# Where the last tiles of a routed block collect their expert parts: twelve tiles' loads on SyncE by counted pairs, and the late block's down products among the last pairs

## The reference

```python
x = x + tanh(g_xattn) * cross_attention(layernorm(x), ctx_768, mask)
topk_idx, topk_w = router(layernorm(x))               # 6 of 32 experts for each token
h   = relu2(einsum('th,eih->tei', xn, up_w)) * combine[:, :, None]
moe = einsum('tei,ehi->th', h, down_w)                 # routed experts, 128 wide inside
shared = relu2(xn @ shared_up_w.T) @ shared_down_w.T   # 512 wide inside
x = x + tanh(g_ffn) * (moe + shared)
```

## Time and profile before

| | us |
|---|---|
| median of 3 runs (lowest to highest) | 724.94 (724.51 to 725.96) |
| the profiled execution's own time | 724.91 |
| its span in the profile | 723.0 |
| PE busy in the span | 675.8 (93%) |
| DVE busy | 523.6 (72%) |
| ACT busy | 454.5 (63%) |
| POOL busy | 475.1 (66%) |
| mean DMA rate | 200 GB/s |

### The profile page before, as it was taken

The page is one execution under the profiler, slowest core; times in us unless marked ns, Lnnn a source line. Parts: engine busy times, 40 slices in busy tenths (PEclk is TensorE's granted clock), DMA queues, the critical chain, the costliest instruction groups (busy, mean ns, idle before and its releaser), DMA issues.

```text
span 723.0 us, 18770 instructions
## 1 busy us (share of the span) xinstructions
PE 675.8 (93%) x5928; PEld 570.4 (79%) x5928; DVE 523.6 (72%) x1782; ACT 454.5 (63%) x1299; POOL 475.1 (66%) x478
## 2 busy tenths in 40 slices
PE   7999998899898989889999899999999999999975
PEld 6888887778787878765674799998899888898854
DVE  2676788787878787876473566666568888888887
ACT  1567757688887878782524765656775576665740
POOL 1455442667566666667777777777777777777764
PEclk9999999999999999999999999999999999999997
DMA  8990000252222222443838986666679999999866
GB/s 296 381 285 3 2 2 23 74 213 95 90 94 88 88 96 88 145 155 127 326 118 282 317 279 212 211 192 191 200 238 325 346 351 345 348 352 343 257 202 232
DMA packets 86305, 144.80 MB, mean 200 GB/s; under 512 B 14646, under 2 KB 60993, under 8 KB 85184
## 3 DMA queue, kind: packets, MB, share of 16 engines
q1 hardware_dynamic: 54288, 71.23, 31.3%
q0 software_dynamic: 19968, 52.34, 19.4%
q10 hardware_dynamic: 11952, 20.03, 8.3%
HBM read 78.00 MB, written 69.73 MB: 204 GB/s over the span
## 4 chain that ended last, share of the span: by engine, by line
PE 49%; DVE 23%; ACT 9%; DVEq 9%; issue 6%; DMA 2%; SPq 1%; ACTq 0%
PE ps L1560 8%; PE ps L1575 8%; PE ps L1416 5%; PE ps L1363 5%; PE ps L1546 4%; DVEq L1178 4%; PE ps L1214 3%; PE ps L1334 3%; PE ps L1447 3%; ACT big L606 3%; PE ps L1326 2%; ACT att L606 2%; DMA big<-in_x_t 2%; PE ps L1428 2%; DVE big L1159 2%
## 5 line engine op out<-in xcount | busy, mean ns | idle before, releaser
L470 POOL DMA_INDIRECT routed_rows<-x_n,slots x120 | 122.2, 1019 | 66.8 <-issue 24.8
L560 POOL DMA_INDIRECT token_parts<-hid,place x112 | 115.8, 1034 | 37.5 <-issue 31.7
L1560 PEld LDWEIGHTS ps<-att 128*128 128x128 f32 x768 | 99.9, 191 | 17.4 <-issue 10.3
L712 ACT ACTIVATE att<-ps 128x512 f32<-128x512 f32 x96 | 57.3, 597 | 82.5 <-PE ps L1546 77.7
L1560 PE MATMUL ps<-att 128*128 128x128 f32 x768 | 102.0, 276 | 4.1 <-DVE att L1142 2.1
L606 ACT ACTIVATE att<-ps,nmax,rstd 128x154 f32<-128x154 f32 x176 | 82.9, 502 | 21.7 <-DVE nmax L843 16.1
L725 ACT ACTIVATE att<-big 128x256 f32 x224 | 80.3, 408 | 2.6 <-issue 2.2
L1575 PE MATMUL ps<-big,att 128*128 x300 | 78.3, 384 | 3.3 <-DVE picked L1151 2.9
L1334 PE MATMUL ps<-att,big 64*64 64x128 f32 x1536 | 62.2, 282 | 8.5 <-ACT att L623 3.7
L623 ACT ACTIVATE att<-ps 128x512 f32<-128x512 f32 (+1 forms) x96 | 48.1, 544 | 31.1 <-PE ps L1326 31.1
L1214 PE MATMUL ps<-big,hid 128*128 128x128 f32 x512 | 62.8, 276 | 2.0 <-DMA big<-in_x_t 1.3
(11 more groups left out here) (268 smaller groups left out, 1529.6 us busy)
## 6 DMA issues: line engine op xcount, KB each, us to landing
mid<-routed_rows SPq DMA_DIRECT2D x168, 138.0 KB
big<-token_parts ACTq DMA_DIRECT2D x48, 256.0 KB
routing<-routed_rows SPq DMA_DIRECT2D x56, 138.0 KB
x_n<-token_parts ACTq DMA_DIRECT2D x24, 256.0 KB
routed_rows<-pad_row SPq DMA_DIRECT2D x1, 4416.0 KB
routed_rows<-pad_row SPq DMA_DIRECT2D x32, 138.0 KB
x_all<-in_x SPq DMA_DIRECT2D x4, 1024.0 KB, 12.8
big<-in_x_t SPq DMA_DIRECT2D x4, 1024.0 KB, 14.1
```

The source lines that it names most:

```text
L470: nc.gpsimd.indirect_dma_start(rows, bass.IndirectOffsetOnAxis(ap=slots[:, t, k:k + 1], axis=0), normed(t), None).then_inc(s_sca[t // TB % ...
L560: nc.gpsimd.indirect_dma_start(parts, bass.IndirectOffsetOnAxis(ap=place[:, p // 2 % 8, p % 2 * 2 + j:p % 2 * 2 + j + 1], axis=0), y_sb[p ...
L712: A.activation(xt(p), ps[:, p % 2, :], ACT.Copy).then_inc(s_xts, 1)
L1560: ins = M(ps[:, 2 + p % 2, j * P:(j + 1) * P], w_up[p % 2][:, j, c * P:(c + 1) * P], xt(p)[:, j * 256 + c * P:j * 256 + (c + 1) * P], star ...
```

## The change

- **Loads.** `PART_LOAD` is every second pair from 51 on, for tiles 0 to 29 (51, 53, ..., 109). Tiles 0 to 19 stay on ACT. Tiles 20 to 29 are loaded by SP: 20 to 26 stand among its row loads, behind those of the pair eight ahead; 27, 28 and 29 behind all rows. `N_LAST` is 2: tiles 30 and 31.
- **Counts.** Five counts of eight numbers are read in place of two: ahead of tile 20 (the rows of tiles up to 23), of 24 (up to 25), of 26 (up to 27), and two in a row behind tile 26 (up to 29, and all). They come from a product of the table with ones: five small products more on PE in the table stage; DVE's work for it is some instructions fewer.
- **Shared expert.** 32 tasks in place of 28 among the pairs: `SHARED_STEP` spaces the first 28 by 10/3 in place of 11/3 pairs, and block 7's `down_late` follow at 104, 106, 108 and 110. Up to pair 53 that is 14 tasks (10, 13, 16, 20, 23, 26, 30, 33, 36, 40, 43, 46, 50, 53) where 12 stood (10, 13, 17, 21, 24, 28, 32, 35, 39, 43, 46, 50).

```diff
-PART_READY = {0: DONE[1], EARLY: DONE[2], 12: DONE[3], 16: DONE[4], 20: DONE[5]}
-PART_LOAD = {DONE[1] + 5 + 11 * t // 5: t for t in range(24)}
-PART_LOAD.update({103 + 2 * i: 24 + i for i in range(4)})
+PART_READY = {0: DONE[1], EARLY: DONE[2], 12: DONE[3], 16: DONE[4]}
+PART_LOAD = {DONE[1] + 5 + 2 * t: t for t in range(SEG_END[8])}
-N_LAST = NT - SEG_END[7]
+N_LAST = NT - SEG_END[8]
-SHARED_STEP = {10 + 11 * k // 3: task for k, task in enumerate(LATE)}
+SHARED_STEP = {10 + 10 * k // 3 if k < 28 else 2 * k + 48: task for k, task in enumerate(LATE)}
...
+            def wait_scattered(need):
+                for j in range(8):
+                    sp.wait_ge(s_ys[j], need[j])
             def load_parts(t):
+                if t in SEG_END[4:7]:
+                    wait_scattered(load_counts(SEG_END.index(t) - 3))
                 sp.wait_ge(s_fin, t - 2)
...
                     store(PART_LOAD[p - STORE_LAG])
-            need = load_counts(1)
-            for j in range(8):
-                sp.wait_ge(s_ys[j], need[j])
-            for t in range(SEG_END[5], SEG_END[7]):
-                load_parts(t)
-            need = load_counts(0)
-            for j in range(8):
-                sp.wait_ge(s_ys[j], need[j])
+                if PART_LOAD.get(p - AHEAD, 0) >= SEG_END[4]:
+                    load_parts(PART_LOAD[p - AHEAD])
+            need_most, need_all = load_counts(4), load_counts(5)
+            stored = STORED
+            for p, t in PART_LOAD.items():
+                if p + AHEAD >= N_PAIRS:
+                    while stored < t - 3:
+                        store(stored)
+                        stored += 1
+                    if t == SEG_END[7]:
+                        wait_scattered(need_most)
+                    load_parts(t)
+            wait_scattered(need_all)
...
+            for a, at, cols in ((1, 480, 4), (2, 484, 2)):
+                for i in range(a):
+                    M(ps[0:2, 5, at:at + cols], tiles_bf[:, i, :], ones_bf[:, 0:cols], start=i == 0, stop=False, skip_group_check=True)
+                M(ps[0:2, 5, at:at + cols], tiles_f[0:n, a, :], cst[0:n, C_CUM + NE - 1:C_CUM + NE * cols:NE], start=False, stop=True,
...
-            pe.wait_ge(s_xts, N_PAIRS)
-            for t in range(NT - TB, NT):
-                down_late(t)
```

More of the change, by code:

```diff
@@ L72 @@
 assert (TOPK * P * EARLY - NE * (P - 1)) // P >= 2 * EARLY_PAIRS
-PART_READY = {0: DONE[1], EARLY: DONE[2], 12: DONE[3], 16: DONE[4], 20: DONE[5]}
-PART_LOAD = {DONE[1] + 5 + 11 * t // 5: t for t in range(24)}
-PART_LOAD.update({103 + 2 * i: 24 + i for i in range(4)})
+PART_READY = {0: DONE[1], EARLY: DONE[2], 12: DONE[3], 16: DONE[4]}
+PART_LOAD = {DONE[1] + 5 + 2 * t: t for t in range(SEG_END[8])}
 STORED = sum(p + STORE_LAG < N_PAIRS for p in PART_LOAD)
-N_LAST = NT - SEG_END[7]
-LATE = [(i, s) for i in range(FULL, NBLK) for s in range(8) if i >= GAP or s >= 4][:-TB]
-SHARED_STEP = {10 + 11 * k // 3: task for k, task in enumerate(LATE)}
+N_LAST = NT - SEG_END[8]
+LATE = [(i, s) for i in range(FULL, NBLK) for s in range(8) if i >= GAP or s >= 4]
+SHARED_STEP = {10 + 10 * k // 3 if k < 28 else 2 * k + 48: task for k, task in enumerate(LATE)}
 LAST = NBLK - 1
@@ L212, in flamingo_block @@
         end_i = sb("end_i", [1, NE], I32)
-        used = x_n1[:, 0, 0:N_TILES + 16]
-        need_i = sb("need_i", [1, 16], I32)
+        tiles_by = x_n1[:, 0, 0:6]
+        turn = x_n1[:, 0, 8:16]
+        need_i = sb("need_i", [1, 6 * 8], I32)
         flat = hid[:, :, :, :].rearrange("p a s n -> p (a s n)")
@@ L315, in x2t_bank @@
             return 5 if j == 0 else 4
-        def down_bank(t):
-            return 5 if t < NT - TB else (0, 1, 4, 5)[t % 4]
         def ring_row(p):
@@ L392, in store, with load_counts @@
                 sp.dma_start(out_tiles[t], x_all[:, t, :]).then_inc(s_st, 16)
-            def load_counts(which):
-                low, high = ((NT * TOPK, N_PAIRS), (SEG_END[7] * TOPK, DONE[7]))[which]
+            def load_counts(w):
+                low, high = SEG_END[4 + w] * TOPK, (DONE + [N_PAIRS])[4 + w]
                 sp.wait_ge(s_need, 1)
-                return [sp.value_load(need_i[0:1, 8 * which + j:8 * which + j + 1], min_val=32 * ((low + 15 - 2 * j) // 16),
+                return [sp.value_load(need_i[0:1, 8 * w + j:8 * w + j + 1], min_val=32 * ((low + 15 - 2 * j) // 16),
                                       max_val=32 * ((2 * high + 15 - 2 * j) // 16)) for j in range(8)]
+            def wait_scattered(need):
+                for j in range(8):
+                    sp.wait_ge(s_ys[j], need[j])
             def load_parts(t):
+                if t in SEG_END[4:7]:
+                    wait_scattered(load_counts(SEG_END.index(t) - 3))
                 sp.wait_ge(s_fin, t - 2)
@@ L420, in _ @@
                     store(PART_LOAD[p - STORE_LAG])
-            need = load_counts(1)
-            for j in range(8):
-                sp.wait_ge(s_ys[j], need[j])
-            for t in range(SEG_END[5], SEG_END[7]):
-                load_parts(t)
-            need = load_counts(0)
-            for j in range(8):
-                sp.wait_ge(s_ys[j], need[j])
+                if PART_LOAD.get(p - AHEAD, 0) >= SEG_END[4]:
[11 more added lines that the diff above has]
+            wait_scattered(need_all)
             for i in range(N_LAST):
                 sp.dma_start(sums[:, i, :, :].rearrange("p k d -> p (k d)"), part_tiles[NT - N_LAST + i]).then_inc(s_pl2[i], 16)
-            for u in range(STORED, NT - N_LAST):
+            for u in range(stored, NT - N_LAST):
                 store(u)
@@ L762, in _ @@
                     hidden_late(*SHARED_STEP[p])
-                if p in PART_LOAD and PART_LOAD[p] < SEG_END[5]:
+                if p in PART_LOAD and PART_LOAD[p] < SEG_END[4]:
                     load_parts(PART_LOAD[p])
@@ L918, in add_late @@
                 dve.wait_ge(s_dn2, t - TB * FULL + 1)
-                V.scalar_tensor_tensor(x_all[:, t, :], ps[:, down_bank(t), t % 2 * D:(t % 2 + 1) * D], tanh_g[:, 1:2], x_all[:, t, :],
+                V.scalar_tensor_tensor(x_all[:, t, :], ps[:, 5, t % 2 * D:(t % 2 + 1) * D], tanh_g[:, 1:2], x_all[:, t, :],
                                        ALU.mult, ALU.add).then_inc(s_acc2, 1)
@@ L1102, in _ @@
             V.tensor_copy(exp_i[:], ps[0:1, 5, 256:256 + N_TILES])
+            V.tensor_copy(tiles_by[0:1, :], ps[0:1, 5, 480:486])
+            V.tensor_scalar(turn[0:1, :], iota_e[0:1, 0:8], -2.0, 15.0, ALU.mult, ALU.add)
             dve.drain()
             V.tensor_scalar(row_i[:], tile_key[0:1, :], -1.0, None, ALU.add).then_inc(s_row, 1)
[L1105 to L1111, removed]
+            V.tensor_tensor(need_i[:].rearrange("p (w j) -> p w j", w=6), turn[0:1, :].unsqueeze(1).broadcast_to([1, 6, 8]),
+                            tiles_by[0:1, :].unsqueeze(2).broadcast_to([1, 6, 8]), ALU.add)
             dve.drain()
@@ L1186, in _ @@
                 g = sums[:, i, :, :]
-                add_late(t)
                 dve.wait_ge(s_pl2[i], 16)
@@ L1442, in down_late @@
                     pe.wait_ge(s_h, t + TB)
-                if TB * FULL < t <= NT - TB:
+                if t > TB * FULL:
                     pe.wait_ge(s_acc2, t - TB * FULL)
@@ L1446, in down_late @@
                 for s in range(4):
-                    ins = M(ps[:, down_bank(t), t % 2 * D:(t % 2 + 1) * D], h[:, s, t % TB * P:(t % TB + 1) * P], down_sh[:, s, :],
+                    ins = M(ps[:, 5, t % 2 * D:(t % 2 + 1) * D], h[:, s, t % TB * P:(t % TB + 1) * P], down_sh[:, s, :],
                             start=s == 0, stop=s == 3, skip_group_check=True)
@@ L1520, in _ @@
             ins.then_inc(s_cum, 1)
+            for a, at, cols in ((1, 480, 4), (2, 484, 2)):
+                for i in range(a):
+                    M(ps[0:2, 5, at:at + cols], tiles_bf[:, i, :], ones_bf[:, 0:cols], start=i == 0, stop=False, skip_group_check=True)
+                n = TABLES[a][1]
+                M(ps[0:2, 5, at:at + cols], tiles_f[0:n, a, :], cst[0:n, C_CUM + NE - 1:C_CUM + NE * cols:NE], start=False, stop=True,
+                  skip_group_check=True)
             up(3, 0)
```

## The result

| | kernel before | changed kernel |
|---|---|---|
| median of 4 runs (lowest to highest), us | 725.45 (724.51 to 726.29) | 737.32 (735.16 to 739.90) |
| ratio to before (95% interval) | | 1.0155 (1.0126 to 1.0184) |
| time and span of the profiled execution | 724.91 and 723.0 | 739.90 and 738.1 |

The change makes the kernel 1.5% slower, some 12 us. The direction was predicted, the size was not: the forecast was 731.7, and the range ended at 736. One thing first, so that the profile is read rightly: the profiled execution is the slowest of the four. DVE starts pair 0 at 406.88 us in it, and at 402.75 before; 3.25 of these 4.1 us were already there at 340 us and arose in the first 30, which hold no instruction of the change.

What follows compares the result with a forecast made beforehand. DVE's pace was taken to bound the kernel from about pair 55, PE's before. For DVE's end: 720.9 + 0.6 + 1.9 - 0.4 - 1.5 - 1.1 = 720.4, + 2.1 + 5.2 = 727.7; time 731.7 us, range 727 to 736.

Steps and rivals of the forecast that it cites:

- Table stage: Before pair 0, where PE is the chain: five small products more, three bfloat16 and two float32, cost +0.6 us.
- Two tasks more ahead of pair 54: PE reaches pair 54 3.4 us later, DVE wins back 1.55: +1.9; one late add gone ahead: -0.4.
- The end: Waits for a down product behind the loop (-1.5) and for tile 24 (-1.1) go; moved adds gain nothing.
- step 4: SP's count reads delay part loads: DVE waits 2.1 us for tile 20 and 5.2 for tile 27.
- The anchor: First loads behind the counts of tiles 20, 24 and 26 go out 10.05 us after pairs 90, 98, 102 begin.
- covered: Row loads, 5 us late behind each count, run eight pairs ahead (over 20 us), so they cost DVE no wait.
- the rival of full queues: DMA queues full, PE slow: landings stay 8.3 us, waits 4.8 for tile 20, 9.0 for 27; about 737, chance 0.08.
- its premise that DVE's work is kept: Same 32 tiles of parts and 20 late adds, so only shifts of DVE's start and its waits were counted.
- Hidden reads: Rival: SP's count reads are hidden, tiles 20 and 27 arrive in time; 724.4 us, no change, chance 0.09.
- Faster tail: Rival: DVE has slack in the loop, so the 6 us moved from the end vanish there; about 718, chance 0.05.
- The rule that was weighed: Shared DMA engines agree with moving loads from ACT to SP free; small sequencer time opposes read waits, leaving 724.4.

Runs made afterwards that it cites:

- the first experiment: The changed kernel with all forty of SP's count reads moved ahead, one behind each row load of pairs 48 to 87: 726.85 us, ratio 1.0019 to the kernel before.

## Why the prediction was right or wrong

The forecast for DVE's end was 727.7; measured 735.68 in the profile. In the time it was 731.7 against a median of 737.32.

1. *Table stage, +0.6.* Too large, and small: the chain has the five products in 0.31 us.

```profile
384.71 0.10 PE ps L1527
384.80 0.05 PE ps L1529 x2
...
384.90 0.12 PE ps L1529 x2
```

Ahead of pair 0 the profiled execution is 3.5 us later than the forecast counts, 4.13 in place of 0.6. Of this 3.25 is the start of this execution and 0.5 the first expert products, which PE ran slowly:

```profile
405.19 1.66 PE L1570 MATMUL ps<-big,att 128*128 128x128 f32 x8 [1.55 <-ACT att L733]
```

The eight took 1.13 before. Pair 0 began anywhere from 402.75 to 406.88 in the eleven profiles of this study, whatever the kernel, so beyond the 0.31 none of it is put down to the change.

2. *Two tasks more ahead of pair 54: right.* DVE began pair 54 at 548.84 and pair 55 at 551.67:

```profile
547.95 0.48 DVE L927 SCALAR_TENSOR_TENSOR x_all<-ps,tanh_g,x_all 128x256 f32<-128x256 f32 x1 [1.04 <-PE ps L1451]
548.84 0.42 DVE L1145 TENSOR_SCALAR hot<-ps 128x256 f32<-128x256 f32 x1 [0.41 <-PE ps L1570]
...
551.67 0.42 DVE L1145 TENSOR_SCALAR x_n<-ps 128x256 f32<-128x256 f32 x1
```

Against the earlier trace rows that is 7.71 and 6.08 later; without the 4.13 from ahead of pair 0 it is 3.58 and 1.95, forecast 3.4 and 1.9. A task of the shared expert costs its length where PE sets the pace, and the wait that DVE wins back is worth subtracting. The tasks alone cost 1.4 to 1.7 us, and undoing them gave 0.8 to 1.7; each time the effect is near the limit of what the runs can tell.

3. *The end: half right.* The wait for a down product behind the loop is gone, line 927 never waits for line 1451 from 560 on, and two tiles stand in the tail, 2.2 us each:

```profile
730.67 0.42 DVE L1169 TENSOR_TENSOR x_all<-x_all,x_n 128x256 f32<-128x256 f32 x1
731.19 0.96 DVE L1193 TENSOR_TENSOR big<-big 128x768 f32<-128x768 f32 x1
...
733.40 0.95 DVE L1193 TENSOR_TENSOR big<-big 128x768 f32<-128x768 f32 x1
```

Tile 24's wait did not go (1.78 in pair 102), but step 4 had counted such a wait within its 5.2, so the sum holds no error for that.

4. *SP's reads: the mechanism right, the size too small.* This is the step that failed: the waits of 2.1 and 5.2 us in the sum. Forecast were waits of 2.1 and 5.2; measured 1.5 (tiles 20 and 21) and 7.8 (tiles 24, 26, 27), 9.3 in place of 7.3.
   - The anchor failed. The prediction took the first load behind the counts of tiles 20, 24 and 26 to go out 10.05 us after pairs 90, 98 and 102, "the same place", since SP's row loads wait there for DVE. For 90 and 98 it was right (9.6 and 10.1). At pair 102 SP did not wait for DVE: it had not yet worked off tile 24's count. The 4.6 us of a count were weighed against the 20 us that the row loads run ahead, and "covered" was right for the rows, for which DVE never waited; but the lead that they lose is missing at the next count, four pairs on. The experiment with only tile 24's count moved shows it: there tile 27 goes out 20.4 us after pair 102.
   - The other numbers of that step held. Tile 27's loads went out 10.9 us behind tile 26's (forecast 11.0), it took 4.9 us to the step (4.5), and DVE wanted it 20.6 us after pair 102 (20.4, the waits taken out). 23.5 + 4.9 - 20.6 = 7.8.
   - Tile 20 landed 4.5 us after its issue; the 5.6 I took was too careful. The queues were not full just then: the DMA share is 0.98 from 560 to 680, but 0.73 while tile 20's loads ran (663.9 to 668.4). Tile 21 ran at full share (668.4 to 675) and took 6.6 (668.39 to 675.02). Its wait of 0.98 was not in the forecast.
   - The range was narrower than its own bounds. With 0.9 and 4.8 for tile 20 and 4.0 and 9.0 for tile 27, added to 724.4, they give 729.3 to 738.2, not 728 to 736; the upper end was left to the rival of full queues.

5. *Not in the forecast: DVE's odd iterations.* The step that adds into `x_all` (line 1167, 1162 before) takes 0.48 us in place of 0.42: 26 of 30 times from pair 55 on, where it was 3 of 28 before. All of one shape from 560 to 700, before and then changed (count, busy, mean ns):

```profile
L1162 DVE TENSOR_TENSOR x_all<-x_all,big 128x256 f32<-128x256 f32 x16 | 6.8, 426 | 0.0
```

```profile
L1167 DVE TENSOR_TENSOR x_all<-x_all,big 128x256 f32<-128x256 f32 x16 | 7.7, 480 | 0.0
```

   An odd iteration takes 2.33 in place of 2.27 by this, some 1.6 us over the 26 to 28 of them. This term stood at nothing in the prediction, by its premise that DVE's work is kept: the number of instructions is kept, their length is not. It is in the experiments without waits for parts too (23 of 30 at 0.48 with all reads ahead, 18 of 30 with the loads on ACT), and the tasks alone do it 9 of 28 times. So it comes in part with the tasks and in part with the rest of the change; what does it was not tried, and stays open.

Together, against the forecast for DVE's end: 3.5 ahead of pair 0, 2.0 waits, 1.6 odd iterations, and 0.9 in pieces under 0.5, among them more idle times of 0.2 to 0.5 without a named cause; 8.0 in all. The last two, 2.5 in sum, would also explain that the first experiment stands at 726.85 and not at the 724.4 that the sum gives without new waits. With the 3.5 set aside, 2.0 + 1.6 + 0.9 explain 4.5 of the 5.6 us between the forecast and the median 737.32; the rest of 1.1 lies in executions that left no profile, and would fit such starts, which is argued and not shown. With either the waits or the odd iterations at their forecast the median would have been near 735.5, inside the range; it took both.

*The rivals.* Hidden reads: fallen, by moving them (10.5 us) and by doubling them (24 more). Full queues and a slow PE: the time came out nearest to this rival's 737, yet its mechanism is wrong. Tiles 20, 26 and 27 came 4.5 to 4.9 us after their issue, tile 24 5.2 and tile 21 6.6, none 8.3, and the first experiment moves the same bytes with no wait. The slow clock is there (0.59 from 720 on) and costs nothing, as no instruction of DVE waits for PE behind tile 27. A time that lies near a rival's number is no evidence for it. Faster tail: none of the moved work vanished in the loop. From pair 55 to its end DVE took 184.0 us with 9.3 of waits, and 175.3 with 2.6 before: without them 174.7 against 172.7, longer and not 6 shorter.

*The rule that was weighed.* The Trainium skill (DMA: Bandwidth & Descriptors, "Issuing engines are not separate DMA queues") has DMAs of all engines on the same 16 DMA engines. The runs agree: from ACT or from SP, 728.17 and 728.08. It calls the time that a sequencer needs to initiate DMAs usually small. Issuing was small here as well (1.3 us for the three loads of a tile); what was not small are the register reads ahead of them, 4.9 us a count, as long as the 4.5 to 4.9 from the issue to DVE's step. The page speaks of the initiating alone and is not contradicted; the reads are another kind of work on the same sequencer, and they cost 10.5 us.

## What to carry to other kernels

Count an in-order queue's work between two of its gates and set it beside the pace of the engine that opens them. Where it is longer, each later place is late by the difference, however far the queue once ran ahead; the first anchor that the trace gives holds only for the first such block. And register reads belong where the queue idles, once and early: nothing else had to change to win 10.5 us back.

## What the runs showed of the hardware that was not expected

- A count of eight numbers, read into registers with its range checks, takes SP 4.9 us up to the next load (697.52 to 702.37), about 0.6 us a number; three DMA issues take 1.3.
- The same 128x256 add of DVE takes either 0.42 or 0.48 us. From pair 55 on 3 of 28 are long in the kernel before, 9 of 28 with the tasks alone, 18 of 30 with the loads on ACT and 26 of 30 in the changed kernel. The cause was not found.
- In the first 30 us the same sixteen products took 2.05 us in one execution and 3.78 in another, at a granted clock of 1.00 and 0.89 over these 30 us. Kernels that differ only late in the program began pair 0 up to 4 us apart (402.96 with the parts two pairs earlier, 406.88 in the changed kernel), so a difference under that between two single profiles must be placed in the program before it is explained.
